# The router's passes over more slots, a bank for each of the first four score tiles, a reordered opening, in a kernel for attention and a mixture of experts

## The chip, the cores and the metric

The kernel runs on one core of one Trainium2 chip, in one launch. The metric is the device time of one execution in microseconds (us), the median of several. A core has TensorE (PE, matrix products into PSUM), VectorE (DVE), ScalarE (ACT), GpSimd (POOL), SyncE (SP, which here only starts DMAs) and 16 DMA engines. Each engine runs its own list of instructions strictly in order and waits on semaphores that others raise. PSUM has 8 banks of 128 x 512 fp32.

## The reference

The input is `x`, 2 x 1024 tokens of 256 numbers in fp32. Both branches start from a LayerNorm of it, and the result is their sum with the input. Cut to what matters:

```python
xn = layernorm(x)
# attention, 16 heads of 128, causal
z = layernorm(xn) * ln_g + ln_b
q, k, v = rope(z @ wq.T + bq), rope(z @ wk.T + bk), z @ wv.T + bv
a = softmax(causal(q @ k.T / sqrt(128))) @ v @ wo.T + bo + xn
# router: 32 experts in 4 groups, top 2 groups, top 4 experts, 128 slots for each expert
scores = sigmoid(xn @ gate_w.T)                  # 2048 x 32
sc = scores + gate_bias
group = top_2(sc in groups of 8).sum             # 2048 x 4; keep the experts of the best 2 groups
idx = top_4(sc where its group is kept)
w = scores[idx] / (scores[idx].sum + 1e-20) * 2
slot = running count of each expert's tokens, in order of the tokens (slots beyond 127 dropped)
experts: silu(xe @ w1) * (xe @ w3) @ w2          # w1, w3: 256 x 128, w2: 128 x 256
shared = silu(xn @ shared_gate) * (xn @ shared_up) @ shared_down
y = x + a + (weighted sum of experts) + shared
```

## The kernel before

**Precision.** An fp32 product is made of three fast products: each operand is split into a rounded high part and the low rest (names ending in `h` and `l`), and PE computes high x high (L301), low x high (L302), high x low (L303). So each product needs a high part, mostly from ACT, and a low part, from DVE or POOL. The transposes (L440, `turn`) bring probabilities and outputs into the layout that the next product needs.

**The opening** (0 to 77.8 us) works on the tokens in 4 groups of 512 (4 tiles of 128 each): the two LayerNorms (POOL takes the root in `root_of`, DVE statistics and scaling, ACT `zz`), the router's logits and the shared MLP. Its PSUM uses go through the banks 0 to 3 (`pro_uses`, freed by `pro_free`); PE's list is written out by hand (L557 to L619), with dummy products (`idle`, L558) where it would wait.

**The units.** After that come 32 units, n = 4g + j, one for a head of a batch, 28 to 31 us each. PE's list of a unit is the same everywhere: the 8 causal score tiles `scores(n, t)` (128 rows by (t+1) x 128 columns), and between them the transposes `turn(n, 0..11)`, the products with v (`weighted`), the output projection of the unit before (`outproj`), the q and k projections of the next (`project`), and those of v. Most results go through a ring over the banks 4 to 7, of which a bank is freed when ACT, DVE or POOL has read it (`take`, `emptied`); the score tiles lie in banks 0 to 3, in two pairs, even tiles in banks 0-1, odd ones in 2-3. For a tile, DVE adds the mask and finds the row's maximum (`maxes`, L1499), ACT makes the exponentials (`exps`, L1036), PE transposes them, ACT and DVE split them (L1047, L1509). `scores(n, t)` waits for the exponentials of the tile before last.

**Rope.** For each of the 4 parts of a unit's q and k: ACT adds the bias (`rope_in`, L827 and L831), SP swaps halves by two DMAs (L720, L721), POOL multiplies and adds (L1635, L1636, L1639), ACT rounds (`rope_hi`, L840), POOL takes the low part (`rope_lo`, L1157).

**The router** runs on DVE in pieces, between the work of the units: `route(n, at)` is called in unit n at three places: 0 behind `maxes(n, 3)`, 1 behind `maxes(n, 4)`, 2 in front of `maxes(n, 7)`. Before, the pieces are numbered by k = 3n + at. Eight transposes of masks on PE (`masks`) lie between the router's marks and its running count (`route_scan`). From unit 13 on, one pair of experts is worked on in each unit (`E_FIRST`).

## Time and profile before

| | us |
|---|---|
| median of 3 runs | 1035.99 (1035.69 to 1036.99) |
| the profiled execution | 1035.71 |
| its span, first to last instruction | 1033.60 |
| time around the span | 2.11 |
| opening, to the first score tile's matmul | 77.8 |
| units 0 to 12 / 13 to 28 | 364.3 / 498.8 |
| busy PE, DVE, ACT, POOL | 98%, 70%, 64%, 74% |

A row of the timeline has the start in us, how long the instruction (or the run of like ones, `x4`) took, the engine and line, what it writes and reads, its shape, and in brackets how long the engine was idle before it and whose result ended that. Line numbers are those of the kernel before. A matmul's busy time reaches to the modelled end of its pipeline, so PE's idle time is shown a little shorter than what a wait moves.

### The profile page before, as it was taken

The numbers are of one execution on the slowest core, as the hardware profiler recorded it, in microseconds if no ns is written. First come the engines' busy times: TensorE is split into PE (matmuls) and PEld (weight loads), VectorE is DVE, ScalarE is ACT, GpSimd is POOL, SyncE is SP. The second block draws the span as 40 slices with busy tenths as digits, with TensorE's granted clock in tenths as the row PEclk, the third lists the DMA queues.
The fourth block names the chain that finished last, engine by engine and source line by source line (L and its number), as shares of the span: only waits on it lengthen the run. The fifth ranks groups of instructions, "written<-read, shape, count | busy, mean of one in ns | idle before, by whom it ended". The sixth has DMA issues, their size and how long they took to land.

```text
span 1033.6 us, 18758 instructions
## 1 busy us (share of the span) xinstructions
PE 1015.4 (98%) x6464; PEld 906.9 (88%) x6464; DVE 723.0 (70%) x1747; ACT 659.4 (64%) x1450; POOL 769.0 (74%) x655
## 2 busy tenths in 40 slices
PE   8999999999999999999999999999999999999998
PEld 4787888998989898898999899999998999999887
DVE  7968878778786877666666565666666666665666
ACT  5767656666666666666665666766566665666664
POOL 4848776768776875769788687886779788687874
PEclk9999999999999999999999999999999999999999
DMA  6312426211121221232332232423233322231232
GB/s 228 83 57 47 123 52 113 62 43 44 40 62 36 56 53 32 62 84 70 88 96 52 67 88 70 103 55 78 68 91 83 87 76 63 67 83 29 45 102 82
DMA packets 51645, 75.42 MB, mean 73 GB/s; under 512 B 12256, under 2 KB 29024, under 8 KB 51424
## 3 DMA queue, kind: packets, MB, share of 16 engines
q1 hardware_dynamic: 45888, 67.40, 24.3%
q0 software_dynamic: 5392, 6.56, 4.1%
q8 instruction: 53, 0.87, 0.4%
q14 instruction: 40, 0.33, 0.1%
q10 hardware_dynamic: 272, 0.26, 0.1%
HBM read 33.94 MB, written 10.90 MB: 43 GB/s over the span
## 4 chain that ended last, share of the span: by engine, by line
PE 84%; DVE 7%; POOL 4%; ACT 2%; DMA 1%; issue 1%; SPq 0%; DVEq 0%; POOLq 0%; ACTq 0%
PE ps L301 23%; PE ps L303 23%; PE ps L302 23%; PE ps L440 10%; PE ps L523 3%; PE ps L535 1%; DVE ps L1499 1%; POOL qb L1639 1%; POOL qb L1635 1%; POOL qs L1636 1%; DMA qs<-qb 1%; ACT prob L1036 1%; DVE st L1212 1%; DVE rb_ L1425 0%; DVE ptd_l L1509 0%
## 5 line engine op out<-in xcount | busy, mean ns | idle before, releaser
L1635 POOL TENSOR_TENSOR qb<-qb,k_sb 128x512 f32<-128x512 f32 x128 | 171.7, 1342 | 183.0 <-DMA qs<-qb 182.7
L1499 DVE CUSTOM_DVE_ANT_0 ps<-ps,maskr 128x128 f32<-128x128 f32 (+7 forms) x256 | 193.5, 762 | 57.3 <-PE ps L303 57.0
L1036 ACT ACTIVATE prob<-ps,nmax 128x128 f32<-128x128 f32 (+7 forms) x256 | 190.5, 744 | 62.3 <-DVE nmax L1499 60.8
L1047 ACT ACTIVATE ptd_h<-ps 128x128 fp32r<-128x128 f32 (+3 forms) x256 | 108.5, 436 | 169.1 <-PE ps L440 168.4
L1509 DVE TENSOR_TENSOR ptd_l<-ps,ptd_h 128x128 fp32r<-128x128 f32 (+3 forms) x256 | 124.4, 486 | 82.7 <-ACT ptd_h L1047 79.8
L1639 POOL TENSOR_TENSOR qb<-qb,qs 128x512 f32<-128x512 f32 x128 | 166.1, 1298 | 18.7 <-POOL qs L1636 0.4
L1636 POOL TENSOR_TENSOR qs<-qs,k_sb 128x512 f32<-128x512 f32 x128 | 175.7, 1373 | 0.0
L440 PE MATMUL ps<-k_sb,prob 128*128 128x128 f32 x1152 | 171.7, 273 | 4.0 <-DVE ptr_l L1509 1.9
L440 PEld LDWEIGHTS ps<-k_sb,prob 128*128 128x128 f32 x1152 | 135.7, 141 | 19.7 <-issue 4.0
L301 PE MATMUL ps<-k_h,q_h 128*128 128x512 f32 (+3 forms) x384 | 140.9, 367 | 1.9 <-ACT prob L1036 1.8
L1539 DVE SCALAR_TENSOR_TENSOR acc<-ps,rinv,acc 128x256 f32<-128x256 f32 x256 | 111.6, 477 | 29.4 <-PE ps L303 27.8
L303 PE MATMUL ps<-k_h,q_l 128*128 128x512 f32 (+3 forms) x384 | 131.2, 342 | 0.0
L302 PE MATMUL ps<-k_l,q_h 128*128 128x512 f32 (+3 forms) x384 | 131.1, 341 | 0.0
L301 PE MATMUL ps<-x2h,wqh 128*128 128x512 f32 x256 | 108.8, 425 | 1.4 <-DVE x2l L1170 0.6
L303 PE MATMUL ps<-x2h,wql 128*128 128x512 f32 x256 | 100.8, 394 | 0.0
L302 PE MATMUL ps<-x2l,wqh 128*128 128x512 f32 x256 | 100.2, 391 | 0.0
L1509 DVE TENSOR_TENSOR ptr_l<-ps,ptr_h 128x512 fp32r<-128x512 f32 x128 | 87.9, 687 | 6.0 <-ACT ptr_h L1047 2.6
L1047 ACT ACTIVATE ptr_h<-ps 128x512 fp32r<-128x512 f32 x128 | 76.0, 594 | 16.2 <-PE ps L440 15.5
L301 PE MATMUL ps<-ptd_h,v_h 128*128 128x256 f32 (+3 forms) x258 | 84.8, 329 | 0.0
L301 PEld LDWEIGHTS ps<-k_h,q_h 128*128 128x128 f32 x384 | 72.6, 189 | 12.5 <-ACT prob L1036 5.0
L303 PE MATMUL ps<-ptd_h,v_l 128*128 128x256 f32 (+3 forms) x258 | 83.0, 322 | 0.0
L1157 POOL TENSOR_TENSOR q_l<-qb,q_h 128x512 fp32r<-128x512 f32 x62 | 81.1, 1307 | 2.0 <-ACT q_h L840 1.5
(193 smaller groups left out, 2599.4 us busy)
## 6 DMA issues: line engine op xcount, KB each, us to landing
qs<-qb SPq DMA_DIRECT2D x256, 128.0 KB, 2.3
ew<-epack SPq DMA_DIRECT2D x16, 768.0 KB, 4.3
rqk<-wqk SPq DMA_DIRECT2D x16, 256.0 KB, 3.0
rv<-wvp SPq DMA_DIRECT2D x8, 256.0 KB, 3.1
ro<-wop SPq DMA_DIRECT2D x16, 128.0 KB, 2.8
token_table<-xn SPq DMA_DIRECT2D x4, 512.0 KB, 4.5
token_sum<-token_table SPq DMA_DIRECT2D x1, 2048.0 KB, 9.4
token_sum<-x POOLq DMA_DIRECT2D x1, 2048.0 KB, 16.4
```

Source lines behind the costliest of these rows:

```text
L301: eng.matmul(dst, lhs[0], rhs[0], start=start, stop=False)
L302: eng.matmul(dst, lhs[0], rhs[1], start=False, stop=False)
L303: return eng.matmul(dst, lhs[1], rhs[0], start=False, stop=stop)
L440: ins = pe.transpose(bank[:, j * P:(j + 1) * P], prob[:, t % 2, (j0 + j) * P:(j0 + j + 1) * P], ident)
L1036: act.activation(prob[:, t % 2, 0:w], tile[t], ACT.Exp, bias=nmax[:, t:t + 1], scale=-1.0, accum_out=rsum[:, t:t + 1]).then_inc(exp_done, 1)
L1047: act.activation(turned(0, t, j0, w), src, ACT.Copy).then_inc(pth_done, 1)
L1499: dve.tensor_tensor_reduce(out=tile[t], in0=tile[t], in1=maskr[:, SEQ - w:SEQ], scale=-1.0, scalar=3e38, op0=ALU.add, op1=ALU.min, accum_o ...
L1509: dve.tensor_tensor(turned(1, t, j0, w), src, turned(0, t, j0, w).bitcast(F32), ALU.subtract).then_inc(ptl_done, 1)
L1539: ins = dve.scalar_tensor_tensor(out=acc[:, t, :], in0=rbank("OP", u, c, i2)[:, i * DM:(i + 1) * DM], scalar=rinv[:, j:j + 1], in1=acc[:, ...
L1635: pool.tensor_tensor(qb[:, i, :], qb[:, i, :], cos_sb[:, c], ALU.mult).then_inc(rope_a, 1)
L1636: pool.tensor_tensor(qs[:, i % 2, :], qs[:, i % 2, :], sin_sb[:, c], ALU.mult).then_inc(rope_b, 1)
L1639: pool.tensor_tensor(qb[:, i, :], qb[:, i, :], qs[:, i % 2, :], ALU.add).then_inc(rope_t, 1)
```

## The change

It does six things.

- **Banks.** Each of the score tiles 0 to 3 gets a bank of its own. `scores(n, 1)` and `scores(n, 3)` wait for no exponentials; `scores(n, 2)` waits for tile 7 of the unit before where it waited for `exps(n, 0)`; `scores(n, 4)` waits for `exps(n, 1)` where it waited for `exps(n, 2)`. The others wait as before.
- **Router.** The pieces lie in other slots and some are cut in two. Unit by unit after the change, at 0 / 1 / 2: units 0 to 3 scores(q) / - / best(q); 4 groups / equal / -; 5 order and chosen / - / mask; 6 top, three quarters / the fourth / index, one quarter; 7 index, the rest / onehot / onehot; 8 onehot twice / marks / marks; 9 marks twice / - / sums; 10 scan half / inverse / weights; 11 scan half / - / want and find; 12 find / take; 13 slots in 1. The four copies of the marks go from DVE (`route_four`) to ACT (`marks_four`, four of 128 x 512). Experts start in unit 14 instead of 13.
- **Rope.** `rope_hi(n + 1, 3)` moves on ACT from the end of unit n to behind `exps(n + 1, 1)`.
- **Loads.** The first 512 rows of x come in four DMAs of 128 KB instead of two of 256 KB, each with its own semaphore.
- **Opening's head.** POOL gets one more small `tensor_scalar` in front of the first root; PE has 13 dummy products instead of 16 in front of the transposes of `zz`.
- **Opening's end.** `scores(0, 0)`, `maxes(0, 0)` and `exps(0, 0)` go in front of the last two down projections and what reads them, on PE, DVE and ACT.

```diff
@@ -54,2 +54,2 @@
-E_FIRST = 13
-MASKS = 8
+E_FIRST = 14
+MASKS = 9
@@ -100,7 +100,8 @@
-        tile = [score[t % 2][:, P * (t == 4):P * (t == 4) + (t + 1) * P] for t in range(TILES)]
+        tile = [ps[:, t, 0:(t + 1) * P] if t < 4 else score[t % 2][:, P * (t == 4):P * (t == 4) + (t + 1) * P]
+                for t in range(TILES)]
@@ -415,11 +416,11 @@
             def scores(n, t):
                 if n not in range(UNITS):
                     return
-                if n == 0 and t in (0, 1, 4, 5):
-                    i = 2 * (t % 2) + t // 4
-                    pe.wait_ge(pro_free[i], len([u for u in range(len(pro_uses)) if u % 4 == i]))
-                if not (n == 0 and t < 2):
-                    pe.wait_ge(exp_done, TILES * n + t - 1)
+                if n == 0 and t < 4:
+                    pe.wait_ge(pro_free[t], len([u for u in range(len(pro_uses)) if u % 4 == t]))
+                elif t not in (1, 3):
+
+                    pe.wait_ge(exp_done, TILES * n + {0: -1, 2: 0, 4: 2, 5: 4, 6: 5, 7: 6}[t])
...
@@ -545,8 +546,7 @@
-                if q == 0:
-                    pe.wait_ge(m4_ready, 2)
+                pe.wait_ge(m4_ready, q + 1)
@@ -561,7 +561,7 @@
             turn_tiles(xn, "xt", xn_tile, xn_ready)
-            idle(16)
+            idle(13)
             turn_tiles(zz, "zt", z_tile, z_ready)
@@ -614,12 +614,14 @@
             gate_turn(3)
+            scores(0, 0)
             down(3, 0)
             down(3, 1)
             pe.wait_ge(maskb_ready, 1)
 
             for n in range(UNITS):
-                scores(n, 0)
+                if n:
+                    scores(n, 0)
@@ -722,7 +724,8 @@
-            sp.dma_start(xt[:, 0, 0:2, :], x_t[0][:, 0:2, :]).then_inc(x_in[0], 16)
+            sp.dma_start(xt[:, 0, 0, :], x_t[0][:, 0, :]).then_inc(x_in[0], 16)
+            sp.dma_start(xt[:, 0, 2, :], x_t[0][:, 2, :]).then_inc(x_part[1], 16)
@@ -776,7 +779,7 @@
-                if n == MASKS + 1:
+                if n == MASKS + 2:
@@ -944,7 +947,8 @@
-            act.dma_start(xt[:, 0, 2:4, :], x_t[0][:, 2:4, :]).then_inc(x_half, 16)
+            act.dma_start(xt[:, 0, 1, :], x_t[0][:, 1, :]).then_inc(x_part[0], 16)
+            act.dma_start(xt[:, 0, 3, :], x_t[0][:, 3, :]).then_inc(x_part[2], 16)
@@ -1087,13 +1089,29 @@
+            def marks_four(n, q):
+
+                if n != MASKS:
+                    return
+                act.wait_ge(mk_ready, q + 1)
+                t = slice(q * GT, (q + 1) * GT)
+                act.activation(m4[:, t, :].rearrange("p t (g e) -> p t g e", g=GROUPS),
+                               mk[:, t, :].unsqueeze(2).to_broadcast([P, GT, GROUPS, EXPERTS]), ACT.Copy).then_inc(m4_ready, 1)
+
+            exps(0, 0)
+            shared_out(3, 0)
+            shared_out(3, 1)
             for n in range(UNITS):
                 g = n // 4
-                exps(n, 0)
+                if n:
+                    exps(n, 0)
                 turned_hi(n - 1, 11)
                 expert_out(n - 1)
                 exps(n, 1)
+                if n:
+                    rope_hi(act, n, 3)
                 rope_in(act, n + 1, 1)
+                marks_four(n, 1)
...
@@ -1139,7 +1160,6 @@
                 if n:
                     v_hi(act, n, 2)
-                rope_hi(act, n + 1, 3)
@@ -1207,8 +1227,8 @@
-                    if (q, s, i) == (0, 0, 2):
-                        dve.wait_ge(x_half, 16)
+                    if q == s == 0 and i:
+                        dve.wait_ge(x_part[i - 1], 16)
                     ins = dve.bn_stats(st[:, 2 * q + s, i, :], src[:, i, :])
@@ -1400,29 +1423,33 @@
-            def route_four(half):
-                for g in (2 * half, 2 * half + 1):
-                    ins = dve.tensor_copy(m4[:, :, g * EXPERTS:(g + 1) * EXPERTS], mk[:, :, :])
-                ins.then_inc(m4_ready, 1)
...
-            def route_scan():
-                dve.wait_ge(mt_ready, NG)
-                stepped(dve.tensor_tensor_scan(cum, mt[:, :], zcol[:, 0:1].to_broadcast([P, TOK]), 0.0, ALU.add, ALU.add))
+            def route_scan(half):
+
+                t = slice(half * TOK // 2, (half + 1) * TOK // 2)
+                dve.wait_ge(mt_ready, (NG // 2, NG)[half])
+                first = cum[:, TOK // 2 - 1:TOK // 2] if half else 0.0
+                stepped(dve.tensor_tensor_scan(cum[:, t], mt[:, t], zcol[:, 0:1].to_broadcast([P, TOK // 2]), first,
+                                               ALU.add, ALU.add))
@@ -1452,40 +1479,55 @@
             def route(n, at):
 
-                k = 3 * n + at
...
-                elif k == 9:
+                elif n == 5 and at == 0:
                     route_order()
-                elif k == 10:
+                    route_chosen()
+                elif n == 5 and at == 2:
                     route_mask()
...
-                elif k == 23:
+                elif n == MASKS and at == 2:
                     route_sums()
...
-                elif k == 3 * (MASKS + 2):
+                elif n == MASKS + 2 and at == 2:
                     route_find(0)
-                elif k == 3 * (MASKS + 3):
+                elif n == MASKS + 3 and at == 0:
                     route_find(1)
...
@@ -1559,11 +1601,16 @@
+            logits(3)
+            maxes(0, 0)
+            for p in range(2):
+                dve.wait_ge(rows_out[p], 32)
             for n in range(UNITS):
...
@@ -1666,6 +1713,8 @@
             stepped(pool.memset(power[:, :], -0.5))
+
+            stepped(pool.tensor_scalar(var[:, 0, :], power[:, :], EPS, None, ALU.add))
             root_of(0, 0, 1)
```

PE at the end of the opening, before; `swh,shh` and its like are the down projections, `k_h,q_h` the score tiles:

```order
L360 MATMUL ps<-k_sb,lgt 128x64 [waits pro_free1]
L360 MATMUL ps<-k_sb,lgt 128x64 x3
L301 MATMUL ps<-swh,shh 128x256 [waits pro_free2,swl_ready,shl_ready]
L302 MATMUL ps<-swl,shh 128x256
L303 MATMUL ps<-swh,shl 128x256
...
L301 MATMUL ps<-swh,shh 128x256
L302 MATMUL ps<-swl,shh 128x256
L303 MATMUL ps<-swh,shl 128x256
L301 MATMUL ps<-k_h,q_h 128x128 [waits rope_l,pro_free0,maskb_ready]
L302 MATMUL ps<-k_l,q_h 128x128
L303 MATMUL ps<-k_h,q_l 128x128
L301 MATMUL ps<-k_h,q_h 128x256 [waits pro_free2]
```

and after:

```order
L361 MATMUL ps<-k_sb,lgt 128x64 [waits pro_free1]
L361 MATMUL ps<-k_sb,lgt 128x64 x3
L302 MATMUL ps<-k_h,q_h 128x128 [waits rope_l,pro_free0]
L303 MATMUL ps<-k_l,q_h 128x128
L304 MATMUL ps<-k_h,q_l 128x128
L302 MATMUL ps<-swh,shh 128x256 [waits pro_free2,swl_ready,shl_ready]
L303 MATMUL ps<-swl,shh 128x256
L304 MATMUL ps<-swh,shl 128x256
...
L302 MATMUL ps<-swh,shh 128x256
L303 MATMUL ps<-swl,shh 128x256
L304 MATMUL ps<-swh,shl 128x256
L302 MATMUL ps<-k_h,q_h 128x256 [waits pro_free1,maskb_ready]
```

The three products of the first score tile now stand behind the transposes of the logits (L360, after L361) and in front of 24 products of the two down projections; the second score tile stays behind them.

DVE from the end of unit 11 into unit 12, before; L1499 is the maximum of tile 7, L1522 the low part of the output that PE transposes next:

```order
L1539 SCALAR_TENSOR_TENSOR acc<-ps,rinv,acc 128x256 [waits op_done]
L1539 SCALAR_TENSOR_TENSOR acc<-ps,rinv,acc 128x256
L1509 TENSOR_TENSOR ptd_l<-ps,ptd_h 128x128 [waits pth_done]
L1499 ISA ps,nmax<-ps,maskr 128x1024 [waits s_done]
L1499 ISA nmax 128x1
L1509 TENSOR_TENSOR ptr_l<-ps,ptr_h 128x4x128 [waits pth_done]
L1509 TENSOR_TENSOR ptd_l<-ps,ptd_h 128x2x128 [waits pth_done]
```

and after:

```order
L1581 SCALAR_TENSOR_TENSOR acc<-ps,rinv,acc 128x256 [waits op_done]
L1581 SCALAR_TENSOR_TENSOR acc<-ps,rinv,acc 128x256
L1551 TENSOR_TENSOR ptd_l<-ps,ptd_h 128x128 [waits pth_done]
L1458 TENSOR_SCALAR m8<-k_sb 128x16
L1459 MAX_INDEX i8<-m8,rb_ 128x8 [waits vec_step]
L1541 ISA ps,nmax<-ps,maskr 128x1024 [waits s_done,vec_step]
L1541 ISA nmax 128x1
L1551 TENSOR_TENSOR ptr_l<-ps,ptr_h 128x4x128 [waits pth_done]
L1551 TENSOR_TENSOR ptd_l<-ps,ptd_h 128x2x128 [waits pth_done]
```

The first half of the search in the running counts (want, L1458, and find, L1459) now stands right in front of the maximum of tile 7.

ACT from the end of unit 3 into unit 4, before:

```order
L1047 ACTIVATE ptd_h<-ps 128x3x128 [waits t_done]
L840 ACTIVATE q_h<-qb 128x512 [waits s_done,rope_t]
L1047 ACTIVATE ptr_h<-ps 128x4x128 [waits t_done]
L1036 ACTIVATE prob,rsum<-ps,nmax 128x128 [waits max_done]
L1047 ACTIVATE ptd_h<-ps 128x4x128 [waits t_done]
L1036 ACTIVATE prob,rsum<-ps,nmax 128x256 [waits max_done]
L827 ACTIVATE qb<-ps,bqs 128x512 [waits rope_l,p_done]
L1047 ACTIVATE ptd_h<-ps 128x128 [waits t_done,pv_done]
```

and after:

```order
L1049 ACTIVATE ptd_h<-ps 128x3x128 [waits t_done]
L1049 ACTIVATE ptr_h<-ps 128x4x128 [waits t_done]
L1038 ACTIVATE prob,rsum<-ps,nmax 128x128 [waits max_done]
L1049 ACTIVATE ptd_h<-ps 128x4x128 [waits t_done]
L1038 ACTIVATE prob,rsum<-ps,nmax 128x256 [waits max_done]
L843 ACTIVATE q_h<-qb 128x512 [waits s_done,rope_t]
L830 ACTIVATE qb<-ps,bqs 128x512 [waits rope_l,p_done]
L1049 ACTIVATE ptd_h<-ps 128x128 [waits t_done,pv_done]
```

`q_h` (L840, L843 after) is `rope_hi` of part 3. It now stands behind the exponentials of tiles 0 and 1 of the new unit, right in front of the next `rope_in`.

## Rows read from the trace of the kernel before

**Rows 1.** Stretches: us, busy (x) of PE, PEld, DVE, ACT, POOL, clock, DMA, GB/s.

```profile
10.90:17.00 6.10, 6.04 (x25) 2.79 (x24) 5.92 (x25) 4.15 (x9) 3.93 (x9) 0.72 0.86 315
77.70:123.20 45.50, 43.15 (x251) 36.79 (x251) 37.43 (x110) 30.56 (x69) 35.61 (x29) 1.00 0.32 81
151.90:182.20 30.30, 28.59 (x182) 25.53 (x181) 25.45 (x62) 19.47 (x43) 20.73 (x16) 1.00 0.63 113
238.90:268.00 29.10, 28.58 (x182) 25.49 (x181) 22.57 (x46) 18.06 (x42) 23.76 (x20) 1.00 0.17 39
296.30:356.40 60.10, 58.72 (x378) 51.72 (x377) 46.41 (x94) 39.81 (x87) 45.73 (x34) 1.00 0.23 53
413.10:442.10 29.00, 28.64 (x182) 25.55 (x182) 19.58 (x48) 18.43 (x42) 22.73 (x20) 1.00 0.29 69
442.10:940.90 498.80, 498.80 (x3252) 454.34 (x3252) 315.75 (x751) 318.03 (x711) 391.95 (x336) 1.00 0.30 76
995.20:1033.60 38.40, 33.56 (x239) 30.74 (x238) 25.05 (x59) 17.94 (x42) 22.58 (x11) 1.00 0.16 56
```

**Rows 2.** Timeline, PE at the end of unit 2.

```profile
154.03 0.41 PE L440 MATMUL ps<-k_sb,prob 128*128 128x128 f32 x2 [1.16 <-DVE ptr_l L1509]
```

**Rows 3.** Timeline, PE: score tile 2 of units 12 and 31.

```profile
417.49 0.45 PE L301 MATMUL ps<-k_h,q_h 128*128 128x384 f32 x1 [0.36 <-ACT prob L1036]
...
1001.27 0.44 PE L301 MATMUL ps<-k_h,q_h 128*128 128x384 f32 x1 [0.65 <-ACT prob L1036]
```

**Rows 4.** Timeline: the sums on DVE in unit 7, waits of PE in unit 8.

```profile
293.01 1.23 DVE L1413 TENSOR_TENSOR sg<-sg,sc 128x512 f32<-128x512 f32 x1
...
298.88 0.30 PE L440 MATMUL ps<-k_sb,prob 128*128 128x128 f32 x1 [0.24 <-DVE ol L1522]
...
305.58 0.47 PE L301 MATMUL ps<-ptr_h,v_h 128*128 128x512 f32 x1 [0.94 <-DVE acc L1539]
```

**Rows 5.** Timeline, PE in unit 0.

```profile
82.55 0.55 PE L440 MATMUL ps<-k_sb,prob 128*128 128x128 f32 x3 [1.01 <-ACT prob L1036]
```

**Rows 6.** Timeline, end of unit 11: POOL, and DVE in front of tile 7.

```profile
409.19 1.30 POOL L1639 TENSOR_TENSOR qb<-qb,qs 128x512 f32<-128x512 f32 x1
...
410.78 1.23 DVE L1499 CUSTOM_DVE_ANT_0 ps<-ps,maskr 128x1024 f32<-128x1024 f32 x1 [0.91 <-PE ps L303]
```

**Rows 7.** Lines: duration ns min/median/max, first and last start us, shape.

```profile
L1432 DVE FIND_INDEX8 i<-m,rb_ x2: 2285/2286/2286, 366.3 to 396.2; 128x8 uint32<-128x2048 f16 x2
L1431 DVE TENSOR_SCALAR m<-k_sb x1: 1181/1181/1181, 365.0 to 365.0; 128x16 f16<-128x16 f32 x1
L1440 DVE TENSOR_SCALAR cnt<-cnt x1: 175/175/175, 402.3 to 402.3; 128x16 f32<-128x16 f32 x1
L1425 DVE TENSOR_TENSOR_SCAN rb_<-ra_,zcol x1: 4674/4674/4674, 339.0 to 339.0; 128x2048 f16<-128x2048 bf16 x1
L1384 DVE TENSOR_TENSOR sc<-sc,gg x1: 1722/1722/1722, 171.5 to 171.5; 128x512 f32<-128x512 f32 x1
```

**Rows 8.** Timeline, the first LayerNorm: DVE, POOL.

```profile
4.36 1.41 DVE L1212 BATCH_NORM_STATS2 st<-xt 128x6 f32<-128x256 f32 x4 [2.67 <-DMA xt<-x]
...
6.38 0.77 POOL L1653 TENSOR_SCALAR var<-mv 128x4 f32<-128x4 f32 x1 [5.55 <-DVE mv L1215]
...
12.23 0.24 POOL L1653 TENSOR_SCALAR var<-mv 128x4 f32<-128x4 f32 x1 [3.95 <-DVE mv L1215]
```

**Rows 9.** Timeline, ACT and PE at the end of the opening.

```profile
74.43 0.76 ACT L917 ACTIVATE ztmp<-ps,cols_sb 128x512 f32<-128x512 f32 x1
...
74.78 0.39 PE L301 MATMUL ps<-swh,shh 128*128 128x256 f32 x1
```

**Rows 10.** Timeline, POOL and ACT around the start of unit 25.

```profile
819.09 1.27 POOL L1157 TENSOR_TENSOR q_l<-qb,q_h 128x512 fp32r<-128x512 f32 x1
...
822.30 0.68 ACT L827 ACTIVATE qb<-ps,bqs 128x512 f32<-128x512 f32 x1
...
826.01 1.29 POOL L1635 TENSOR_TENSOR qb<-qb,k_sb 128x512 f32<-128x512 f32 x1 [2.96 <-DMA qs<-qb]
```

More of the change, by code:

```diff
@@ L201, in layer @@
         small_in, rqk_in, rv_in, ro_in = sem("small_in"), sem("rqk_in"), sem("rv_in"), sem("ro_in")
-        sw_in, x_half = [sem(f"sw_in{i}") for i in range(3)], sem("x_half")
+        sw_in, x_part = [sem(f"sw_in{i}") for i in range(3)], [sem(f"x_part{i}") for i in range(GT - 1)]
         xn_tile, z_tile, pow_ready, first_ready = (sem(s) for s in ("xn_tile", "z_tile", "pow_ready", "first_ready"))
@@ L1347, in _ @@
             shared_lo(3, 1)
-            logits(3)
-            for p in range(2):
-                dve.wait_ge(rows_out[p], 32)
             def route_scores(q):
@@ L1370, in route_groups, with route_equal @@
                 own = gs[:, :, :].unsqueeze(3).to_broadcast([P, NT, GROUPS, GROUPS])
[L1371 removed]
+                stepped(dve.tensor_tensor(gcmp[:, :, :, :], other, own, ALU.is_gt))
+            def route_equal():
+                other = gs[:, :, :].unsqueeze(2).to_broadcast([P, NT, GROUPS, GROUPS])
+                own = gs[:, :, :].unsqueeze(3).to_broadcast([P, NT, GROUPS, GROUPS])
                 stepped(dve.tensor_tensor(geq[:, :, :, :], other, own, ALU.is_equal))
```

93 lines of the change are left out of this document (57 added, 36 removed).

## The prediction

> **What bounds the kernel now.** I read the stretches first, from unit to unit, since the share of a whole span hides where the idle time is. In units 13 to 28 PE is busy for 498.80 of 498.80 us [rows 1]: nothing that the change does there can gain, and everything can only cost. The idle time of PE lies in units 0 to 12, in the last two units and in the opening. For each of these stretches I then looked in the timeline for the rows of PE that carry an idle time in brackets, and asked what ended it. Two kinds come out. In the first, a score tile waits for exponentials: tile 2 of units 12 and 31 starts 0.36 and 0.65 late behind `exps(n, 0)` [rows 3]. In the second, DVE is held by a router piece and the low part or the maximum that PE needs comes late: at the end of unit 2 PE is idle for 1.16 behind `ptr_l` [rows 2], which stands on DVE behind the maximum of tile 7 and the groups' piece. The experts' units have no router pieces, and no waits.
>
> **A scale for the waits.** An idle time in brackets is smaller than what a wait moves. From start to start of the matmuls, against the same pair in an undisturbed unit, the 1.16 is 1.33, the 0.36 is 0.53 and the 0.24 of [rows 4] is 0.40. I use the bracket plus 0.17 for each wait; this is read from those three, and an estimate for the others.
>
> **What goes.** By stretch, PE's length minus its busy time [rows 1]:
> - 77.70 to 123.20 (units 0 and 1): 2.35. Of it 1.01 is the transpose at 82.55 behind the exponentials of tile 2 [rows 5]; its chain of tile, maximum and exponentials is unchanged. The other 1.34 lies in six small waits behind the three score pieces of unit 0; the change leaves one such piece and one of the best two in unit 0.
> - 151.90 to 182.20 (units 2 and 3): 1.71, two waits, behind the groups' piece and the mask's piece. Both pieces are cut and moved. The groups' first part comes in place 0, where a scan of 4.67 [rows 7] passed with a wait of 0.2 at most (the 1.38 of the stretch 296.30 to 356.40, less the 0.94 and the 0.24 of [rows 4]).
> - 238.90 to 268.00 and 413.10 to 442.10: 0.52 and 0.36, both tile 2, which now waits for a result that is there some 5 us earlier. The same in unit 31, 0.65 [rows 3].
> - 296.30 to 356.40: 1.38. The 0.94 at 305.58 belongs to the masks' way through the ring [rows 4] and moves with them to unit 9, so I count the other 0.44.
>
> That is 1.34 + 1.71 + 0.52 + 0.36 + 0.65 + 0.44 = 5.02 in 13 waits, and with 13 x 0.17 = 2.2 it is 7.2 us.
>
> **What comes.** Place 2 of an odd unit is where the change puts the mask, the sums and the search. How much DVE can be held there is told by the sums of unit 7: from 293.01 to the maximum's start is 1.95 (1.23 for the product, the rest for the reduction), and PE lost 0.40 behind `ol` [rows 4]. So about 1.5 us is free there: 0.9 in which DVE waits for tile 7 anyway [rows 6], and 0.6 until PE wants `ol`. Then:
> - the mask's product, 1.72 [rows 7]: 1.72 - 1.5 = 0.2;
> - the sums, moved to place 2 of unit 9 unchanged: 0.4 again;
> - want and find, 1.18 + 2.29 = 3.47 with gaps 3.55 [rows 7], in place 2 of unit 11: 3.55 - 1.5 = 2.05. The want is 128 x 16, and a like operation took 0.175 [rows 7]; with that the piece is 2.5 and the cost 1.0. The bounds are 0.9 and 2.1; I take 1.85, nearer to the row of the same line.
> - `scores(0, 0)` at the opening's end waits for the bank that ACT's L917 frees at 74.43 + 0.76 = 75.19 [rows 9]; PE is there at about 74.78, where the down projections begin now. With the way of the signal 0.5, between 0.3 and 0.7. It gives nothing itself, since PE has 24 products for DVE and ACT to be late behind; where the chain of tile 0 was hidden already, the move is only order.
>
> Together 0.2 + 0.4 + 1.85 + 0.5 = 3.0 us.
>
> **What costs nothing.** The copies of the marks on ACT (4 x about 0.6) lie beside a PE that waits for none of them but the masks. The scan's halves, about 2.3 each, are under what place 0 let pass. The search's second half stays in place 0. `rope_hi(n + 1, 3)` comes about 2.5 us later: what is queued behind it on ACT is the next `rope_in`, 0.6 later, whose DMAs POOL waits for, and what waits for it is POOL's low part, which at unit 25 is done at 820.36 where the exponentials of tile 1 end at 822.3; POOL then still waits 2.96 for the swapped halves [rows 10]. That idle time hides 0.6 and the 1.3 of the low part with 1 us over. PE reads part 3 only for tile 4 and later. Without that cover each odd unit would lose what is missing. Experts from unit 14 end in unit 29 instead of 28: unit 29 takes the length that unit 13 gives up.
>
> **The opening's head.** Each tile's statistics (1.41 for four) start when 128 KB are in, where DVE waited 2.67 for 256 KB [rows 8], and POOL's first `tensor_scalar`, 0.77 where the second took 0.24 [rows 8], has a warm predecessor: 0.5. On the other side the shared weights are issued one DMA later (0.43) on SP, and DVE's low part of them stands in front of the Newton step. I take 0.8 off the first LayerNorm, bounds 0 and 1.3, and let it reach the end, as PE's list in the opening is the bound behind it.
>
> **The sum.** -7.2 + 3.0 - 0.8 = -5.0, on the profiled execution's 1035.71 (its span, 1033.60, and 2.11 around it, which the change leaves alone): 1030.7. The median of the runs stands 0.28 above the profiled execution, so 1031.0. The likeliest case's own range is 1029.5 to 1032.6.
>
> [...] POOL's L1639 runs from 409.19 to 410.49, over the place where the want would start, at about 409.86 [rows 6]. The want took 1.18 against 0.175 for a like one [rows 7], which looks like a wait of 1.0 inside the instruction. [...]
>
> **Rivals.**
> - *A larger gain, about 1028.7.* The want falls into a gap of POOL and costs 0.85 less than I take, the head gives its 1.3, and the masks' 0.94 goes, since each mask's transposes now wait for their own copy: 1031.0 - 0.85 - 0.5 - 0.94 = 1028.7. For it: the 0.175 row [rows 7]. Against it: POOL at 409.19 covers the place [rows 6].
> - *Given back, 1034 to 1036.* The router's work on DVE is the same, only ACT takes the copies; the pieces in new slots meet other waits (place 1 of units 4 and 8, the masks in unit 9), so that 3 to 5 of the 7.2 come back. For it: in units 0 and 1 DVE is busy for 37.43 of 45.50 [rows 1], and it stays near that with the same pieces. Against it: the pieces at places 0 and 1 are each shorter than ones which passed there.
> [...]
> - *Slower, 1036.5 to 1039.* The moved `rope_hi` makes POOL late in the units in which nothing is idle on PE. One mechanism: in the odd expert units POOL's chain for the next unit's first parts is the tight one; it decides as soon as the shift (0.6 + what ACT adds) passes the 2.96 less 1.3 of idle time [rows 10]. To cancel 5.0 it needs 0.31 in each of 16 units. Against it: that idle time.
> - *The banks do nothing*, because tile 2 waits for something else next (PE's ring): then 0.52 + 0.36 + 0.65 and 3 x 0.17, 2.0, do not come: 1033.0.
>
> **How the numbers follow.** Forecast 0.60; larger gain 0.10; clock 0.09; banks nothing 0.05; given back 0.11; slower 0.05. No change is within 0.2%, 2.07 us, which a measurement of this kernel can just tell. Faster than 1033.92: forecast, larger, clock and banks, 0.84; given back lies mostly within: 0.10 same; slower 0.06. The range is 1028.4 to 1034.2: below it lies a part of the larger gain, above it most of given back and slower.
>
> **What would show it.** In the profile after: no bracket at tile 2 of any unit; 1.0 or less idle in unit 0 after the tile-2 wait; PE idle near 1.7 in front of the transposes of `ol` at the start of unit 12, and 0.2 and 0.24 in units 6 and 10; an idle time of 0.3 to 0.5 at L302 for tile 0 of unit 0; units 14 to 29 without a wait. It is wrong if the expert units show idle time on PE, if the wait at unit 12 is above 2.5, or if the clock is at half after the first transposes of `zz`.

## The result, and the profile after

The changed kernel takes 1031.9 us (median, 1031.59 to 1032.86), the kernel before 1036.61 (1035.69 to 1037.93) in the same series: a ratio of 0.9957, 95% interval 0.9946 to 0.9967. 1031.0 was predicted, in a range of 1028.4 to 1034.2. Every number is from executions in the fast state; one execution of all those below, 5726.82 us with `rope_hi` behind `rope_in`, was not and is left out of its ratio. The span of the profiled execution fell from 1033.6 to 1029.5, and these are the stretches of the changed kernel that answer to [rows 1] (us, busy (x) of PE, PEld, DVE, ACT, POOL, clock, DMA share, GB/s):

```profile
10.30:16.40 6.10, 5.94 (x22) 2.37 (x21) 5.92 (x25) 4.26 (x9) 3.93 (x9) 0.72 0.98 327
78.00:121.40 43.40, 41.94 (x248) 36.51 (x247) 31.89 (x102) 30.23 (x67) 35.59 (x29) 1.00 0.33 83
149.80:178.00 28.20, 28.20 (x182) 25.55 (x181) 22.34 (x63) 18.68 (x43) 19.80 (x16) 1.00 0.67 121
234.70:263.10 28.40, 28.40 (x182) 25.66 (x182) 20.96 (x68) 18.95 (x42) 23.37 (x20) 1.00 0.19 43
291.40:351.20 59.80, 58.27 (x378) 51.70 (x377) 46.57 (x97) 41.26 (x91) 42.66 (x34) 1.00 0.20 49
407.90:438.10 30.20, 28.78 (x183) 25.60 (x181) 23.27 (x54) 19.25 (x43) 22.84 (x19) 1.00 0.25 49
466.30:963.80 497.50, 497.50 (x3230) 451.63 (x3230) 313.05 (x748) 318.39 (x707) 390.94 (x335) 1.00 0.31 76
991.90:1029.50 37.60, 33.44 (x239) 30.77 (x238) 24.89 (x59) 18.02 (x42) 22.55 (x11) 0.98 0.17 57
```

Units 3 and 6 have lost their idle time altogether, and unit 12 has got 1.42. Units 8 and 9 have 1.53 where they had 1.38. Most of the idle times left are where the prediction put them: at tile 0 of unit 0, at tile 2's transposes of unit 0, behind `acc` (the sum over the heads, on DVE) while the masks pass through the ring in unit 9, and behind the find in unit 12 (two waits, not one). The one at 345.88 is new:

```profile
74.69 0.33 PE L302 MATMUL ps<-k_h,q_h 128*128 128x128 f32 x1 [0.49 <-ACT ztmp L920]
...
82.46 0.55 PE L441 MATMUL ps<-k_sb,prob 128*128 128x128 f32 x3 [1.01 <-ACT prob L1038]
...
330.94 0.47 PE L302 MATMUL ps<-ptr_h,v_h 128*128 128x512 f32 x1 [0.69 <-DVE acc L1581]
...
345.88 0.47 PE L302 MATMUL ps<-x2h,wqh 128*128 128x512 f32 x1 [0.77 <-DVE ptr_l L1551]
...
409.66 0.52 PE L441 MATMUL ps<-k_sb,prob 128*128 128x128 f32 x3 [0.83 <-DVE ptr_l L1551]
...
411.56 0.30 PE L441 MATMUL ps<-k_sb,prob 128*128 128x128 f32 x1 [0.59 <-DVE ol L1564]
```

At 345.88 PE waits for `ptr_l`, the low part of transposed probabilities. DVE does it behind the maximum of tile 6, for which DVE itself waited for PE (0.62), so no router piece holds it; odd units without masks (7 and 11) have no such wait. That the masks' extra use of the ring, now in an odd unit, makes it is my reading of the rows; no run isolates it.

The start of each unit's first score tile on PE, less its start in the kernel before, shows where the time came from. Worked out from the two traces it is -0.05 where the opening ends (at tile 1 of unit 0), -4.22 at unit 4, -4.98 at unit 7, -5.23 at unit 10, -4.04 at unit 13, -5.97 at unit 14, -5.70 at unit 29 and -3.29 at unit 31; after it, the wait at tile 2 of unit 31 gone, -4.1 at the end. One thing in it was not foreseen. From unit 15 (-6.73) to unit 29 (-5.70) the difference shrinks in every unit by a little: a unit of experts takes 31.13 to 31.15 where it took 31.09 and 31.05 in turn, 1.03 in 14 units, though PE is busy for 497.50 of 497.50 us. The first experiments ask for that, and what they found was larger than what was asked.

### The profile page after: what moved, and what is told of

Same layout as the page of the kernel before. It is cut to its first block, busy times and chain, and to the rows that moved or that the text cites. A ratio compares the mean times of both kernels' runs of the same rounds, so it can differ in the third digit from the quotient of the medians.

```text
span 1029.5 us, 18761 instructions
## 1 busy us (share of the span) xinstructions
PE 1014.0 (98%) x6461; PEld 906.7 (88%) x6461; DVE 717.4 (70%) x1746; ACT 664.8 (65%) x1454; POOL 768.8 (75%) x656
## 4 chain that ended last, share of the span: by engine, by line
PE 91%; DVE 4%; POOL 2%; ACT 1%; DMA 1%; issue 0%; SPq 0%; DVEq 0%; POOLq 0%; ACTq 0%
PE ps L302 25%; PE ps L304 25%; PE ps L303 25%; PE ps L441 12%; PE ps L524 3%; PE ps L536 1%; DVE ps L1541 1%; POOL qb L1686 1%; POOL qb L1682 1%; POOL qs L1683 1%; DMA qs<-qb 0%; DMA ra_<-sh_gate 0%; ACT prob L1038 0%; DVE st L1232 0%; PE ps L510 0%
## 5 line engine op out<-in xcount | busy, mean ns | idle before, releaser
L851 ACT ACTIVATE v_h<-ps 128x512 fp32r<-128x512 f32 x64 | 38.3, 598 | 78.3 <-PE ps L304 78.3
```

## The experiments

Twelve further kernels ran, each against the kernel before on the same chip. Ratios are to the kernel before; the changed kernel's is 0.9957. The intervals are 0.0018 to 0.0027 wide, 2 to 3 us: where two of them overlap, the times can't tell the kernels apart, and what a part of the change is worth is read from the traces, one execution of each.

| kernel | median us | ratio (95% interval) | profiled span |
|---|---|---|---|
| changed | 1031.9 | 0.9957 (0.9946 to 0.9967) | 1029.5 |
| rope_hi back at its old place | 1035.78 | 0.9995 (0.9986 to 1.0004) | 1033.0 |
| before, with the banks only | 1033.44 | 0.9976 (0.9966 to 0.9986) | 1030.5 |
| first score tile back | 1032.68 | 0.9966 (0.9954 to 0.9978) | 1031.3 |
| want early | 1031.11 | 0.9949 (0.9935 to 0.9962) | 1028.9 |
| before, with rope_hi moved only | 1035.99 | 1.0002 (0.9992 to 1.0012) | 1035.4 |
| low part of the shared weights late | 1031.83 | 0.9962 (0.9949 to 0.9975) | 1029.5 |
| before, with experts from unit 14 only | 1041.53 | 1.0049 (1.0036 to 1.0062) | 1039.5 |
| rope_hi behind rope_in | 1030.8 | 0.9948 (0.9935 to 0.9961) | 1028.5 |
| the old banks | 1032.82 | 0.9966 (0.9952 to 0.9979) | 1030.7 |
| the old head | 1032.5 | 0.9963 (0.9949 to 0.9976) | 1030.6 |
| combined | 1029.83 | 0.9935 (0.9921 to 0.9948) | 1026.5 |
| combined, with a new head | 1029.79 | 0.9937 (0.9923 to 0.995) | 1027.5 |

### rope_hi back at its old place

```diff
                 exps(n, 1)
-                if n:
-                    rope_hi(act, n, 3)
                 rope_in(act, n + 1, 1)
...
                     v_hi(act, n, 2)
+                rope_hi(act, n + 1, 3)
```

> The changed kernel with rope_hi(n + 1, 3) back at its old place on ACT, at the end of unit n. Theory R (the moved rope_hi is what makes units 15 to 28 longer, 31.14 against 31.05 us: rope_in(n + 1, 1) ends 0.6 later and with it the bank of the ring that turn(n, 1) takes, a wait of 0.06 to 0.09 below what the brackets show): each of these units is 31.05 again, the span 1.2 to 1.3 shorter than 1029.5, time near 1030.6; POOL's idle time in front of L1682 is back from 148 to about 183. Rival (the longer units come from something else, such as DVE's or POOL's later start): units stay at 31.14 and the time at 1031.9. Second rival: the move bought something in units 0 to 12, so that the time is above 1031.9.

It went the other way: 3.9 us slower by the ratio, most of the change's gain, and 3.5 in the span. The units of experts are a little shorter, 31.07, so the small thing was right; but units 14, 20 and 26 are 1.6, 0.6 and 1.3 us longer than in the changed kernel, 3.5 together. The second rival had the sign and a part of the place: units 1, 6 and 8 are 0.35, 0.23 and 0.31 longer, 0.9 of it. The timeline of this kernel at unit 14, ACT and then PE:

```profile
471.37 0.63 ACT L843 ACTIVATE q_h<-qb 128x512 fp32r<-128x512 f32 x1 [2.34 <-POOL qb L1685]
...
472.39 0.36 ACT L1038 ACTIVATE prob<-ps,nmax 128x128 f32<-128x128 f32 x1
...
473.27 0.38 PE L302 MATMUL ps<-woh,oh 128*128 128x256 f32 x1 [0.95 <-DVE ptr_l L1550]
```

and of the changed kernel at the same place:

```profile
469.40 0.37 ACT L1038 ACTIVATE prob<-ps,nmax 128x128 f32<-128x128 f32 x1 [0.37 <-DVE nmax L1541]
...
470.75 0.64 ACT L843 ACTIVATE q_h<-qb 128x512 fp32r<-128x512 f32 x1
```

At the old place ACT stands for 2.34 us at `q_h` until POOL has the rope done, and the transposed probabilities and the exponentials of tile 0 are queued behind it, though they need nothing of it. Moved, `q_h` comes when POOL is long done. The groups by line say it in one row for each kernel (count, busy us, mean ns, idle us just before and what ended it): back at the old place,

```profile
L843 ACT ACTIVATE q_h<-qb 128x512 fp32r<-128x512 f32 x64 | 40.2, 628 | 12.8 <-POOL qb L1685 12.8
```

changed, and before:

```profile
L843 ACT ACTIVATE q_h<-qb 128x512 fp32r<-128x512 f32 x64 | 40.3, 630 | 0.0
```

```profile
L840 ACT ACTIVATE q_h<-qb 128x512 fp32r<-128x512 f32 x64 | 40.2, 628 | 7.2 <-POOL qb L1639 7.1
```

So the wait at tile 2 of unit 12 before the change [rows 3] had a cause one step further back: not the exponentials, but what stood in front of them on ACT. The row is there in the kernel before, 1.5 us ahead of that wait:

```profile
415.97 0.63 ACT L840 ACTIVATE q_h<-qb 128x512 fp32r<-128x512 f32 x1 [0.89 <-POOL qb L1639]
```

The wait of unit 31 is another: ACT has no idle time at `q_h` there.

### Before, with experts from unit 14 only

Why does PE wait in units 14, 20 and 26, when it never did in the experts' units of the kernel before, with the same order on ACT (ACT's own idle time at `q_h` was 0.45 at most there)?

```diff
-E_FIRST = 13
+E_FIRST = 14
```

> The kernel before with nothing changed but the experts from unit 14 instead of 13. Theory (the 3.9 us that the move of rope_hi is worth come from the experts' start in an even unit: the gathers on POOL then make the root of q_h late in units 14, 20 and 26): waits on ACT at q_h grow from 7.2 to about 12 us, PE waits of 0.3 to 1.1 appear in those units, 2.5 to 4 us longer, near 1039.5. Rival (they come from the new banks or the router's slots): no wait in units 14 to 28, the time within 0.7 of 1036.3.

The theory held, and more than it asked: 5.1 us slower by the ratio, 5.9 in the span. ACT's idle time at `q_h` is 12.8 again, 2.33, 1.97 and 1.92 of it in the same three units, and PE waits at tile 2. In unit 14:

```profile
474.46 0.63 ACT L840 ACTIVATE q_h<-qb 128x512 fp32r<-128x512 f32 x1 [2.33 <-POOL qb L1639]
...
475.97 0.44 PE L301 MATMUL ps<-k_h,q_h 128*128 128x384 f32 x1 [1.79 <-ACT prob L1036]
```

Units 14, 20 and 26 take 3.64, 1.35 and 1.3 longer than in the changed kernel. Of the 3.64 this wait is 1.96; the other 1.67 come behind it, where PE's granted clock is at half (0.52 in 477.50 to 481.00). So the 5.9 are not waits alone.

To spread the router over one more unit is thus not free: it moves the experts by one unit, and the change carries that only because `q_h` is out of the way. Why it is every sixth unit stays open; POOL's work of a unit depends on its number in several ways and I did not take these apart.

### Before, with the banks only, and before, with rope_hi moved only

```diff
-        tile = [score[t % 2][:, P * (t == 4):P * (t == 4) + (t + 1) * P] for t in range(TILES)]
+        tile = [ps[:, t, 0:(t + 1) * P] if t < 4 else score[t % 2][:, P * (t == 4):P * (t == 4) + (t + 1) * P]
+                for t in range(TILES)]
...
-                    pe.wait_ge(exp_done, TILES * n + t - 1)
+                elif t not in (1, 3):
+                    pe.wait_ge(exp_done, TILES * n + {0: -1, 2: 0, 4: 2, 5: 4, 6: 5, 7: 6}[t])
```

> The kernel before with nothing changed but the banks of score tiles 0 to 3 and what scores(n, t) waits for. Theory: the waits at tile 2 of units 2, 6, 12, 30 and 31 go (0.21 + 0.69 + 0.53 + 0.21 + 0.63 from start to start) and part of unit 0's (0.4), all other waits stay: 2.3 to 2.7 us shorter, near 1034.1, units 13 to 28 unchanged at 31.05. Rival (the next wait takes its place): under 0.7 us.

As expected. 0.9976: 2.5 us by the ratio, 3.1 in the span, all the waits at tile 2 gone, the experts' units as they were.

```diff
                 exps(n, 1)
+                if n:
+                    rope_hi(act, n, 3)
                 rope_in(act, n + 1, 1)
...
-                rope_hi(act, n + 1, 3)
```

> The kernel before with nothing changed but rope_hi(n + 1, 3) moved behind exps(n + 1, 1) on ACT. The run with it back showed ACT waiting for POOL at q_h (12.8 us in all, 0.0 in the changed kernel, 7.2 in the kernel before), with the exponentials of tiles 0 and 1 queued behind it. Theory (two edits do one job: the wait for exponentials at tile 2 is there because exps(n, 0) stands behind rope_hi): even with the old banks the waits at tile 2 of units 2, 6, 12, 30 and 31 shrink or go (up to 2.3), units 14 to 28 grow by 0.08 each (1.2): 0.5 to 1.3 us faster than before, near 1035.3. Rival (the banks alone remove those waits, the move is worth something only with experts from unit 14): the waits stay and the time is 1.2 longer, near 1037.5.

The profile bears out the mechanism: with the old banks the waits at tile 2 of units 2, 6, 12 and 30 are gone, the one of unit 31 (0.65) stays, so that one is no work of `rope_hi`. The time does not: no gain. Each experts' unit pays 0.05 to 0.08, 0.95 in all, and the runs spread from 1034.29 to 1040.1. The profiled execution, one of the slower ones, shows one thing that can be behind the spread. In unit 3 PE stands for 2.20 us behind DVE's `acc`, where 0.55 stood before, and then its clock is at half for the next matmuls:

```profile
174.99:177.50 2.51, 0.31 (x4) 0.11 (x2) 2.51 (x6) 0.88 (x2) 2.37 (x3) 1.00 0.00 0
178.00:181.50 3.50, 3.50 (x10) 2.73 (x9) 2.66 (x14) 2.98 (x7) 3.00 (x4) 0.51 0.01 2
```

Unit 3 takes 33.61 instead of 30.38. The 1.65 of it ahead of the clock are in two of DVE's rows that are long beside a row of POOL: an operation of a router piece (`gg<-gg`, 1.32 instead of 0.75) and `wvl` (1.77 instead of 0.69):

```profile
173.75 1.35 POOL L1636 TENSOR_TENSOR qb<-qb,k_sb 128x512 f32<-128x512 f32 x1 [1.67 <-DMA qs<-qb]
173.88 1.77 DVE L1183 TENSOR_TENSOR wvl<-rv,wvh 128x512 fp32r<-128x512 f32 x1
```

Without these 3.2 us the span would be 1032.2, an estimate, and 1032.2 is the span of the fastest of the twelve runs. So "no gain" is the median of runs of which some may have met this and some not; only one of them was profiled.

### The old banks in the changed kernel

The same two edits as above, undone in the changed kernel.

> The changed kernel with the old banks of the score tiles and their waits. Theory (banks and the move of rope_hi remove the same waits at tile 2): the waits of units 2, 6, 12 and 30 stay away, only unit 31's 0.63 and about 0.4 to 0.9 in unit 0 are back: 1.0 to 1.5 us longer than the changed kernel, near 1033.2, while the banks alone on the kernel before gave 2.9. Rival (they add): 2.5 to 3 us longer, near 1034.7.

0.9966 against 0.9957, which the times alone can't tell from none. From the traces the spans differ by 1.2: 0.34 is in the head (which is not the banks'), 0.14 in unit 4, and the rest is unit 31's wait:

```profile
998.37 0.44 PE L301 MATMUL ps<-k_h,q_h 128*128 128x384 f32 x1 [0.65 <-ACT prob L1037]
```

So the banks are worth 2.5 to 3 us alone and under 1 beside the moved `rope_hi`. But for unit 31's, the two edits remove the same waits, as the theory had it; my sum had given all of them to the banks.

### rope_hi behind rope_in

```diff
-                if n:
-                    rope_hi(act, n, 3)
                 rope_in(act, n + 1, 1)
+                if n:
+                    rope_hi(act, n, 3)
```

> The changed kernel with rope_hi(n, 3) one place later, behind rope_in(n + 1, 1). Theory (rope_in is 0.63 late behind rope_hi, and the transposes of tile 1 wait 0.08 for its bank): units 15 to 28 are 31.05 to 31.07 instead of 31.14 and nothing else moves, 1.1 to 1.4 us shorter, near 1030.7. Rival (POOL's low part is now so late that it delays the next part's root, or the 0.08 comes from elsewhere): no gain, 1031.9 or more.

As expected in the traces: the units of experts take 31.07 and the span is 1.0 us shorter (the intervals of the two ratios overlap). In the changed kernel, unit 20, `rope_in` (L830) ends at 658.92 and PE's three transposes, of which the last two need the bank that it empties, begin at 658.90 and take 0.58:

```profile
657.72 0.62 ACT L843 ACTIVATE q_h<-qb 128x512 fp32r<-128x512 f32 x1
658.24 0.68 ACT L830 ACTIVATE qb<-ps,bqs 128x512 f32<-128x512 f32 x1
658.90 0.58 PE L441 MATMUL ps<-k_sb,prob 128*128 128x128 f32 x3
```

With the two exchanged:

```profile
657.53 0.68 ACT L830 ACTIVATE qb<-ps,bqs 128x512 f32<-128x512 f32 x1
658.10 0.63 ACT L843 ACTIVATE q_h<-qb 128x512 fp32r<-128x512 f32 x1
658.71 0.49 PE L441 MATMUL ps<-k_sb,prob 128*128 128x128 f32 x3
```

No idle time is shown in either: a wait of 0.09 is within the modelled end of the matmul before, and only the distance from start to start tells it.

### Want early

```diff
-                if half == 0:
-                    stepped(dve.tensor_scalar(want[:, :], k_sb[:, C_CV:C_CV + CG], 1.0, None, ALU.add))
...
+                    route_want()
                     route_inverse()
```

> The changed kernel with the want (DVE tensor_scalar of 128 x 16) in unit 10, place 1, instead of in front of the find in unit 11, place 2. Theory: the find's piece falls from 3.12 to 2.40 us and the two waits behind it (0.99 + 0.75) to 0.9 together: 0.7 to 0.85 us shorter, near 1031.2, and the want takes 0.17 to 1.2 depending on POOL's instruction beside it. Rival (the find alone already delays the maximum of tile 7 past the point at which the whole 1.74 is lost): under 0.3.

As expected: the two waits of unit 12 are 0.26 and 0.75 from start to start where they were 0.99 and 0.75, and the unit is 0.74 shorter. Most of the first went, the second stayed. In the changed kernel the search began so (DVE, and POOL beside it):

```profile
403.92 1.29 POOL L1686 TENSOR_TENSOR qb<-qb,qs 128x512 f32<-128x512 f32 x1
...
404.55 0.69 DVE L1458 TENSOR_SCALAR m<-k_sb 128x16 f16<-128x16 f32 x1
```

The want took 0.69 here and ended at 405.24, where POOL's instruction ended at 405.21. It is the same in all the traces: in eleven of the fourteen POOL was in the midst of an instruction, and the want, 0.22 to 1.22 long (1.18 before), ended 0.02 to 0.04 after it; in the other three POOL stood idle or was within 0.02 of its end, and the want took 0.17.

### The first score tile, and the head

```diff
             gate_turn(3)
-            scores(0, 0)
             down(3, 0)
...
-            logits(3)
-            maxes(0, 0)
...
-            exps(0, 0)
             shared_out(3, 0)
```

> The changed kernel with unit 0's first score tile, its maximum and exponentials back behind the last two down projections. Theory: the wait of 0.49 at tile 0 goes and nothing comes in its place, since what stops PE in unit 0 is tile 2's exponentials: 0.5 us shorter, near 1031.4. Rival (the moved tile takes DVE and ACT work off unit 0 and is part of the 1.8 us that units 0 and 1 gave): 0.3 to 1 us longer, near 1032.5, with waits behind exponentials or ptr_l of unit 0 between 80 and 100 us.

Neither. The time is 0.8 higher, within the overlap of the intervals, and the span 1.8, but most of that lies where this edit does nothing. 1.05 is there before PE comes to the moved tile: the load of `sh_gate` was late, and ACT read it at 7.26 instead of 6.45. Another 0.75 comes in units 3 and 4, of it 0.57 with a wait behind DVE's `acc` that the old head shows too (0.39 there). Between, the moved tile can be read: with it back, tile 1 of unit 0 comes 0.5 earlier against the logits' last transposes, since the wait of 0.49 is gone; but at the start of unit 1 PE waits behind POOL's `q_l` for 0.35 more than the changed kernel does, and at unit 2 no more than 0.1 of the 0.5 is left. So in this one trace the wait at tile 0 costs 0.5 in the opening and 0.4 of it is given back in the next two units, where another wait would have come.

```diff
-            idle(13)
+            idle(16)
...
-            sp.dma_start(xt[:, 0, 0, :], x_t[0][:, 0, :]).then_inc(x_in[0], 16)
-            sp.dma_start(xt[:, 0, 2, :], x_t[0][:, 2, :]).then_inc(x_part[1], 16)
+            sp.dma_start(xt[:, 0, 0:2, :], x_t[0][:, 0:2, :]).then_inc(x_in[0], 16)
...
-            stepped(pool.tensor_scalar(var[:, 0, :], power[:, :], EPS, None, ALU.add))
```

> The changed kernel with the old head: two loads of x, 16 dummies, no extra tensor_scalar on POOL. Theory (the head gives 0.6 and the moved first score tile takes 0.5 of it by its wait for L920's bank, so the head is worth its 0.6 only once): first transposes near 9.2 to 9.5 instead of 8.87, 0.3 to 0.7 us longer, near 1032.4. Rival (the opening is bound elsewhere): no difference, 1031.9.

0.6 us longer by the medians, as expected, and 0.74 later at tile 0 of unit 0 in the profile, with the first transposes at 9.36. It is less sure than it looks: the intervals overlap, and kernels that share the new head and the moved tile reach tile 0 at 74.40 to 75.03, against 75.43 here. Nor is the 0.5 shown to be the extra `tensor_scalar`'s: the nine kernels with it have 0.22 for the first one, but of the five without it three (this one, the banks only, `rope_hi` moved only) have 0.24 too, and only two 0.77 (the kernel before [rows 8], and with the experts from unit 14 only).

```diff
-            shared_lo_w(dve, 0)
             first_root(0)
             norm(0)
             stats(0, 1)
+            shared_lo_w(dve, 0)
```

> The changed kernel with DVE's low part of the first shared weights behind the first normalization and the second statistics instead of in front of the Newton step. Theory (the head's gain is capped by the load of sh_gate: statistics start 0.87 earlier than before, PE's first transposes only 0.60): the transposes at 8.87 come 0.5 to 0.9 earlier, and the end of the opening with them: 0.4 to 0.8 us shorter, near 1031.3. Rival (the head is not the bound, or the clock stays at half for longer): first transposes earlier, first score tile at 74.7 as before, time 1031.9.

The rival had it. The cap was real, the first transposes come 0.75 earlier; but the work behind them is not. On DVE the weights' low part and the next group's statistics both stand between the second statistics and the Newton step now, and `zz` begins at 13.78 instead of 13.92. The 13 dummies, at full clock (1.00 in 9.00 to 12.25), are done by 12.25, PE is idle for 2.18, and behind it the clock is low (0.59 in the second row), where the changed kernel has 1.00 in the same stretch:

```profile
14.43 2.17 PE L336 MATMUL ps<-k_sb,zz 128*128 128x128 f32 x8 [2.18 <-ACT zz L908]
```

```profile
16.20:18.20 2.00, 2.00 (x7) 1.33 (x6) 1.97 (x5) 1.78 (x3) 0.76 (x1) 0.59 0.28 97
```

### Combined

The want early, `rope_hi` behind `rope_in`, and the search out of place 2:

```diff
-                elif n == MASKS + 1 and at == 0:
-                    route_scan(0)
-                elif n == MASKS + 2 and at == 0:
-                    route_scan(1)
-                elif n == MASKS + 2 and at == 2:
+                elif n == MASKS + 1 and at == 0:
+                    route_scan()
+                elif n == MASKS + 2 and at == 0:
                     route_find(0)
```

> The changed kernel with three edits: rope_hi(n, 3) behind rope_in(n + 1, 1), the want in unit 10 place 1, and the scan whole in unit 10 place 0, so that the find's halves stand in place 0 of units 11 and 12 and nothing of the search in place 2. Theory (the terms add): 1.1 from rope, 0.74 from the want, and of the find's remaining waits (0.26 + 0.75) all, against 0.2 to 0.45 for the whole scan: 2.4 to 2.7 us under the changed kernel, near 1029.4, with no wait between 405 and 415. Rival (place 0 is no better for 2.3 us, or the whole scan costs over 1): near 1030.1 or above.

This has the lowest ratio, 0.9935, and a span 3.0 shorter than the changed kernel's, of which 0.3 is the head's. Both waits of unit 12 are gone, and the whole scan costs 0.19. The interval's upper end, 0.9948, just meets the changed kernel's lower one, 0.9946, so that it is faster is likely from the times and plain from the traces.

With the low part of the shared weights late, as above, and 18 dummies:

> The same with the low part of the first shared weights behind the second statistics, and 18 dummy products instead of 13 in front of the transposes of zz. Theory (with the low part late alone, PE stood idle for 2.18 in front of those transposes and ran at half clock behind them, which ate the 0.75 that the first transposes had gained): the idle time is 1.1 or less, the clock stays full behind it, and 0.5 to 0.8 of the head reach the end: near 1028.8. Rival (the dummies run at half clock and end late, or zz is the bound): the same as the combination without it within 0.2.

The idle time in front of `zz` is 1.11 and the clock stays at 1.00 (10.00 to 13.00 and 14.50 to 18.50), as expected, but the transposes of `zz` begin only 0.12 earlier than in the combined kernel and the end of the opening moves by 0.07: the rival again, `zz` is the bound. And this profiled execution lost 1.1 in unit 10, at the scan. That is the clearest pair of rows in the study. Combined:

```profile
359.51 4.42 DVE L1448 TENSOR_TENSOR_SCAN rb_<-ra_,zcol 128x2048 f16<-128x2048 bf16 x1
359.83 5.20 POOL L1678 TENSOR_TENSOR qb<-qb,k_sb 128x512 f32<-128x512 f32 x1 [0.35 <-DMA qs<-qb]
```

with the new head:

```profile
359.42 1.30 POOL L1678 TENSOR_TENSOR qb<-qb,k_sb 128x512 f32<-128x512 f32 x1
359.42 5.58 DVE L1448 TENSOR_TENSOR_SCAN rb_<-ra_,zcol 128x2048 f16<-128x2048 bf16 x1
360.67 5.39 POOL L1679 TENSOR_TENSOR qs<-qs,k_sb 128x512 f32<-128x512 f32 x1
```

In the first the scan starts 0.32 ahead and takes 4.42, and POOL's instruction, 1.3 long alone, takes 5.20 and ends 1.1 after the scan's end. In the second both start at 359.42, POOL's takes its 1.30, and the scan's row is longer by 1.16, about as much. So a whole scan in place 0 costs 0.19 or 1.35, by 0.3 us of phase.

The traces give a measure for place 0 of a unit (behind `maxes(n, 3)`). A scan's row of 4.42, 4.67, 5.20 and 5.58 us (combined, the kernel before, `rope_hi` moved only, combined with a new head) made its unit 0.19, 0.48, 0.98 and 1.35 longer than a like unit without a piece: what is above 4.2 is lost. (The prediction took 0.2 at most for the 4.67.) The halves of the change took 2.28 to 3.42 each (2.29 where POOL's instruction was at its end, 3.42 where one of 1.31 had begun 0.04 before), and cost nothing in any trace; they are the safer choice.

## Why the prediction was right, and where not

Forecast and traces by stretch, in us. The forecast column has the prediction's terms in the stretches that they belong to; the other is worked out from the starts of the units:

| stretch | forecast | traces |
|---|---|---|
| opening, to tile 1 of unit 0 | -0.3 | -0.05 |
| units 0 to 3 | -4.4 | -4.17 |
| units 4 to 7 | -0.5 | -0.76 |
| units 8 to 11 | -0.4 | -0.25 |
| unit 12 | +1.3 | +1.19 |
| first and last of the experts (13, 14, 29, 30) | 0 | -0.27 |
| units 15 to 28 | 0 | +1.03 |
| unit 31 to the end | -0.8 | -0.80 |
| all | -5.1 | -4.1 |

- **The sum.** -5.0 was forecast; the spans of the profiled executions moved by -4.1, their times by -3.95 and the medians by -4.7. The sign, the size and the case (the first) were right. Every stretch with a named term came out within 0.3; the -4.7 of the medians lies nearer to the forecast than the traces do, and that is luck: the median of the kernel before came out 0.6 higher in this series than the 1035.99 that was known.
- **What goes, units 0 to 3.** 3.05 of idle time and 8 x 0.17, 4.4, was forecast; from the end of the opening to unit 4 the difference moved by 4.17. Right in size. About 0.6 of it is not the router's: the kernel with the banks only has 0.64 there. That the router's new slots gave the other 3.5 is read from the waits that went; no run moves the router alone.
- **What goes, tile 2.** 0.52 and 0.65 went as forecast, and the 0.36 of unit 12 too. For units 6 and 12 the reason was incomplete: there it is ACT's wait for POOL at `q_h`, which either edit takes away. Only the 0.65 of unit 31 needs the banks. The credit was given to the banks for all; beside the moved `rope_hi` they are worth under 1 us.
- **What goes, units 8 and 9.** 0.44 was forecast, 0.78 from start to start, and 0.4 back for the sums. The two units are 0.25 shorter. The sums cost nothing, but the new wait of 0.77 took what the others gave.
- **What comes, place 2.** The find cost 0.99 + 0.75 = 1.74 against 1.85; its piece was 3.12 long, and 3.12 - 1.74 = 1.4 is the free time that the sums of unit 7 had given as 1.5. The mask (0.2) and the sums (0.4) cost nothing that the trace shows, so the signs named for units 6 and 10 did not come. The mask's product took 1.23 in its new slot and not the 1.72 of [rows 7], which is under the 1.5. The sums took 2.4, more than before; they stand right behind the wait of 0.77 in unit 9, in which PE falls back and DVE gains room. That this is why they cost nothing is argued, not tested.
- **What comes, tile 0.** 0.49 against 0.5. "It gives nothing itself" was wrong by the one trace that can tell: 0.4 of it comes back in units 0 and 1.
- **The head.** 0.6 against 0.8: `sh_gate` is read at 6.45 instead of 5.70, the cap that was named. The 0.5 for POOL's first `tensor_scalar` can't be credited to the extra one: three of the five kernels without it show 0.24 as well. With tile 0's wait the opening as a whole gives 0.05.
- **The step that failed** is in "What costs nothing", twice. POOL's idle time did hide the later low part, as said; but the 0.6 by which `rope_in` is late also delays a bank of the ring, 0.06 to 0.09 in each unit of experts and 1.03 in all, which is the whole miss of the traces. And "unit 29 takes the length that unit 13 gives up" holds (2.02 for 1.92), but only with the moved `rope_hi`: alone, the experts' start in unit 14 costs 5.1 us by the ratio. The prediction has the two edits as two rows with zero. That each zero came out near zero together is luck: moving `rope_hi` is worth 3.9, most of it because of the experts' start (3.5 in units 14, 20 and 26, 0.9 in units 1, 6 and 8, less 1.0 in the units of experts), and no rival said so. The prediction looked at what waits behind ACT in a unit of experts, and at no row of ACT's own idle time at `q_h`.
- **The want beside POOL.** The prediction read the want's 1.18 as a wait of 1.0 inside the instruction, while POOL's is running. The traces agree: it ended 0.03 us after POOL's instruction here, and 0.02 to 0.04 after it in the ten other traces in which POOL was running. Counted from POOL's end the forecast of the piece would have been nearer than with 3.55: from 409.86 to 410.49 [rows 6] is 0.63, and with the find (2.29) and the gaps (0.1) that is 3.0, or 3.2 if the whole 0.175 comes behind POOL, a cost of 1.5 to 1.7. The piece measured 3.12 and the cost 1.74. The scan's rows show the same between the two engines (5.58 beside POOL's 1.30, and POOL's 5.20 beside 4.42); what makes one wait for the other, no run shows.
- **The clock.** The 0.09 that the chances give to the clock, to its being low over real products, was the author's estimate; the changed kernel's trace does not show it behind the first transposes. In its opening the clock was low over the dummies as before (0.72 in the first row of stretches) and 1.00 in 16.20 to 18.20; at the very end it fell (0.98 in the last row), but only from 1027.00 on, where PE has no row any more (0.84, then 0.50). It did fall over real products in the kernel with the low part late: the 13 dummies ended by 12.25, PE was idle for 2.18, and the clock was 0.51 in 14.40 to 16.20 and 0.59 in 16.20 to 18.20. Half clock stands also behind idle times of 2.20 us (0.51, `rope_hi` moved only) and 1.79 (0.52, the experts from unit 14).

## What to carry to other kernels

An instruction that waits on an engine's in-order list makes everything behind it wait (ACT's 2.34 us at `q_h` in unit 14 held the exponentials of tile 0), and the profile names the last link of that chain: ask of every wait not only who released it, but what that releaser was queued behind. Edits that each look free can be free only together, so test one undone and one alone before giving the credit. On an engine that is always busy, look at distances from start to start, since 0.07 us in each of 14 units never shows as idle time.
